# Moving the layer-norm statistics, the normalised rows and the low parts in a decoder kernel

## The chip, the cores and the metric

The kernel runs on one core of one Trainium2 chip. The metric is the device time of one execution in microseconds (us). A core has five engines with an instruction stream each: TensorE (PE in the profile, PEld for its weight loads), VectorE (DVE), ScalarE (ACT), GpSimd (POOL) and SyncE (SP), which only issues DMAs here. They run independently and wait for each other through counting semaphores.

## The reference

The input `x` is 16 sequences of 128 rows by 256. One decoder layer is computed, in three steps that each add to `x` (written out from the reference, with shapes):

```python
xn = layernorm(x)
q = l2norm(xn @ Wq); k = l2norm(xn @ Wk); v = xn @ Wv; a = sigmoid(xn @ Wg)   # 8 heads of 128
S = a_t[..., None] * S + k_t[..., None] * v_t[None, :]     # over the 128 time steps, per head
o_t = S^T q_t
x = x + concat(o) @ Wo                                     # step 1: gated linear attention
xn = layernorm(x)
scores = xn @ (ctx @ W^T)^T ; x = x + softmax(scores) @ ctx   # step 2: cross attention
xn = layernorm(x)
gate = softmax(mean_t(xn) @ gate_w^T); the 2 best of 8 experts per sequence
x = x + sum_k w_k * (gelu(xn @ Wd_k^T + bd_k) @ Wu_k^T + bu_k)   # step 3: experts
```

## The kernel before, in words

**Groups, units and the tail.** Four sequences form a group `i` (0 to 3, `NG = 4`), and a group is worked through head by head. One head of one group is a unit `n = 8i + h` (0 to 31, `U = 32`); "the third head" is `h == 2`, units 2, 10, 18 and 26, and "the fourth" is `h == 3`, units 3, 11, 19 and 27. A unit makes k, g (the gate alpha), q and v by projections on PE, splits the time recurrence into seven levels of products, and folds them into the output rows `o`. On DVE every level needs a decay (`decay`, `decay_first`, `q_decayed`: lines 690, 697, 707, 724), and on ACT a copy of the parts that don't decay (`carry`, `carry_odd_k`: lines 466, 457). Levels 1 to 4 of unit n+1 are prepared while unit n runs, levels 5 and 6 at the start of unit n itself.

The cross attention and the experts of group `t = i - 1` (the tail) are cut into small parts and woven into the units of group `i`. Each engine has its own function `tail_part(n, place)`, which is called at fixed places of the unit and says what the tail does there. So the order of each engine is written out by hand, and the semaphores only make sure that nobody reads too early.

**Layer norm.** Each of the three normalisations runs in three pieces: `ln_variance` on DVE (statistics of four sequences: lines 660, 665, 668), `ln_power` on POOL (the power -1/2: line 371, tile `rstd`), and `ln_normalize` on DVE (four TENSOR_SCALARs that write `xn`: line 676). PE then transposes `xn` by eight matmuls (line 1235), and ACT copies the result out of PSUM (line 497). "mid" names the rows after the attention (`x_mid`, used by the scores), "x" the next group's input rows, "cross" the rows after the cross attention. The next group's transposed rows are kept as a high and a low part: `xT_upper` on ACT copies the high part to `xnT`, and `xT_lower` on DVE subtracts it from the PSUM rows to get the low part (line 809).

**The PSUM ring.** Nearly all that PE makes goes through four PSUM banks in a fixed order, `ORDER` (built at the function `fill_order`). `fill(name)` on PE waits until the engine that reads the fourth-last entry has freed its bank; which semaphore that is stands in `freed_by` (line 232). In unit 11 the entries are: scores, v(11), g(12), q(12), oT(9), k(13), probsT, xT(0), xT(1), o(10), and in unit 12: cross(0), cross(1), v(12), g(13), q(13), oT(10), k(14), o(11), x3T(0), x3T(1), v(13), g(14). Thus xT(0) waits for ACT's square of q(12), o(10) for ACT's square of k(13), cross(1) and v(12) for the two low parts on DVE, g(13) and g(14) for the scaled output rows `o_sb` of heads 10 and 11 (`o_scaled` on DVE, line 770), and q(13) for DVE's residual of cross(0).

**POOL.** In each unit POOL first makes the reciprocal norms of the k and q rows (lines 379 and 382, from `norm_sq`, which DVE writes at line 753 at the start of the unit). Behind them, in the third head, stand the powers of "mid" and of the next "x". `v_scaled` (line 762) needs the reciprocal norms of the k rows.

**DVE in a unit** (the loop at line 965): `norm_floor` (753), `decay(n, 5)` (690), `decay(n, 6)` (697), `v_scaled(n)` (762), tail "early", first decays of the next unit (707, 713, 718, 724), tail "late", five `keep`s (741), decays 2 to 4 of the next unit (690), tail "mid", `o_scaled(n - 1)` (770), tail "end". **ACT in a unit** (the loop at line 572): wide copies to `attnT`, carry 5, tail "early", alpha, block copies, tail "mid", q, oT, k, the carries 1 and 2 of the next unit, tail "carry", carries 3 and 4, tail "end".

Of the kernel before, what the change touches and what calls it, by code (L numbers as in the profile page):

```python
# [38 lines left out]
def decoder_kernel(nc, x, ctx, ctxT, wq, wk, wv, wg, wo, xwT, gateT, expert, up_b,  # L39
# [5 lines left out]
    NG = B // GB  # L45
# [7 lines left out]
    with ExitStack() as stack:  # L53
# [372 lines left out]
        def _(act):  # L426
# [99 lines left out]
            def tail_part(n, place):  # L526
                i, h = divmod(n, H)
                t = i - 1
                at = (h, place)
                if at == (0, "early") and i >= 2:  # L530
                    gelu(i - 2)
                if t >= 0:
                    if at == (2, "carry"):
                        for c in range(KC):
                            tail_to(rowsT[:, c], ("x2T", t, c), x2T_set)
                    if at == (3, "early"):
                        probs_out(t)
                    if at == (3, "carry"):
                        tail_to(probsT[:].rearrange("p b t -> p (b t)"), ("probsT", t, 0), probsT_set)
                    if at == (4, "end"):  # L540
                        for c in range(KC):
                            tail_to(rowsT[:, c], ("x3T", t, c), x3T_set)
                    if at == (6, "mid"):
                        gate_exp_out(t)
                if at == (3, "end") and i + 1 < NG:
                    xT_upper(i + 1)
                if place == "end" and h in (6, 7):
                    tail_to(projT[:, h - 6].rearrange("p b t -> p (b t)"), ("keys", i, h - 6), keys_set)
                if at == (7, "end") and t >= 0:
                    for z in range(2):  # L550
                        downT_out(t, z)
# [99 lines left out]
        def _(dve):  # L651
# [5 lines left out]
            def ln_variance(name, src):  # L657
                at = NORM_AT[name]
                for b in range(GB):
                    last = nc.vector.bn_stats(stats[:, b], src[:, b])  # L660
                last.then_inc(ln_stat, 1)
                wait_first(ln_stat, 2 * at + 1)
                positive(dve, ln_rstd, at)
                for b in range(GB):
                    last = nc.vector.bn_aggr(mean_var[:, b], stats[:, b])
                last.then_inc(ln_stat, 1)
                dve.wait_ge(ln_stat, 2 * at + 2)
                nc.vector.tensor_scalar(var_eps[:], mean_var[:, :, 1], LN_EPS, None, ALU.add).then_inc(ln_var, 1)
# [11 lines left out]
            def decay(n, l):  # L680
                if n > 0:
                    dve.wait_ge(level_mm, LEVELS * (n - 1) + DONE[l if l < INNER else OUTER])
                dve.wait_ge(decayed, OUTER * n + l - 1)
                dve.wait_ge(carry_set, CARRIES * n + min(l - 1, CARRIES))
                dve.wait_ge(span_set, INNER * n + l - 1)
                if l < OUTER:
                    w = 2 ** (l - 1)
                    by = (view(alpha, 1, [[2, 2], [4, N // 4], [0, 2]]) if l == 2 else
                          view(spans, span_at(l - 1), [[1, 2], [2, N // (2 * w)], [0, w]]))
                    nc.vector.tensor_tensor(halves(l, w, True), halves(l - 1, w, True), by, ALU.mult).then_inc(decayed, 1)  # L690
                else:

                    for operand, at, span in ((0, T - BLOCK, 2), (1, 0, 1)):
                        src, dst = (view(states, tile_q(m) + operand * N + at, [[T, GB], [1, BLOCK]])
                                    for m in (l - 1, l))
                        by = view(spans, span_at(l - 1) + span, [[4, GB], [0, BLOCK]])
                        last = nc.vector.tensor_tensor(dst, src, by, ALU.mult)
                    last.then_inc(decayed, 1)
# [57 lines left out]
            def v_scaled(n):  # L756
                pair, half = n // 2, n % 2
                dve.wait_ge(v_mm, n + 1)
                dve.wait_ge(rk_set, 2 * pair + 2)
                positive(dve, o_mm, 2 * pair - 2)  # L760
                by = view(rnorm, (2 * pair - 2) % 4 * 8 + 4 + 2 * half, [[1, 2], [8, 2], [0, P]])
                nc.vector.tensor_tensor(v_sb[:, pair % 2, 2 * half:2 * half + 2],
                                        ring_of(("v", n))[:].rearrange("p (b h v) -> p b h v", b=2, h=2), by,
                                        ALU.mult).then_inc(v_set, 1)
# [9 lines left out]
            def residual(t):  # L774
                positive(dve, out_free, 16 * 2 * t)
                dve.wait_ge(x_in[t % 2], 16 * (t // 2 + 1))
                for z in range(2):
                    dve.wait_ge(wo_mm, 2 * t + z + 1)
                    nc.vector.tensor_tensor(x_mid[:, 2 * z:2 * z + 2], accs[z][:].rearrange("p (b d) -> p b d", b=2),
                                            x_buf[:, t % 2, 2 * z:2 * z + 2], ALU.add).then_inc(mid_set, 1)  # L780
                dve.wait_ge(mid_set, 2 * t + 2)
# [115 lines left out]
            def tail_part(n, place):  # L897
                i, h = divmod(n, H)
                t = i - 1
                at = (h, place)  # L900
                if at == (0, "late") and i >= 2:
                    weigh_up(i - 2)
                if at == (0, "end") and i >= 2:
                    last_residual(i - 2)
                if t >= 0:
                    if at == (1, "end"):
                        residual(t)
                    if at == (2, "early"):
                        ln_variance(("mid", t), x_mid)
                    if at == (2, "late"):  # L910
                        ln_normalize(("mid", t), x_mid, ("x3T", t - 1, 1) if t > 0 else ("xT", 1, 1))
                    if at == (3, "early"):
                        scores_max(t)
                    if at == (3, "end"):
                        probs_rsum(t)
                    if at == (4, "early"):
                        cross_residual(t)
                        dve.wait_ge(cross_set, 2 * t + 2)
                        ln_variance(("cross", t), x_mid)
                if i + 1 < NG:  # L920
                    if at == (2, "end"):
                        dve.wait_ge(x_in[(i + 1) % 2], 16 * ((i + 1) // 2 + 1))
                        ln_variance(("x", i + 1), x_buf[:, (i + 1) % 2])
                    if at == (3, "late"):
                        ln_normalize(("x", i + 1), x_buf[:, (i + 1) % 2], ("x2T", t, 1) if t >= 0 else ("xT", 0, 1))
                    if at == (3, "end"):
                        xT_lower(i + 1)
                if t >= 0:
                    if at == (4, "late"):
                        ln_normalize(("cross", t), x_mid, ("xT", i + 1, 1) if i + 1 < NG else ("x2T", t, 1))  # L930
                    if at == (5, "late"):
                        pool_rows(t)
                        dve.wait_ge(pooled_set, t + 1)
                        gate_products(t)
                    if at == (6, "early"):
                        gate_logits(t)
                    if at == (6, "late"):
                        choose(t)
                    if at == (6, "end"):
                        choice_weights(t)  # L940
# [24 lines left out]
            for n in range(U):  # L965
                if n >= 1:
                    norm_floor(n - 1)
                decay(n, 5)
                decay(n, 6)
                v_scaled(n)  # L970
                tail_part(n, "early")
                if n + 1 < U:
                    decay_first(n + 1)
                    span_products(n + 1)
                    q_decayed(n + 1)
                tail_part(n, "late")
                for k in range(KEEPS):
                    keep(n, k)
                if n + 1 < U:
                    for l in range(2, INNER):  # L980
                        decay(n + 1, l)
                tail_part(n, "mid")
                if n >= 1:
                    o_scaled(n - 1)
                if n == 0:
                    dve.wait_ge(w_in, N_W)
                tail_part(n, "end")
# [505 lines left out]
```

## Time and profile before

| | us |
|---|---|
| median of 3 runs | 513.37 (513.32 to 513.6) |
| the profiled execution | 512.21 |
| its span, first to last instruction | 510.4 |
| PE busy | 467.0 (92% of the span) |
| DVE busy | 365.9 (72%) |
| ACT busy | 338.2 (66%) |
| POOL busy | 110.3 (22%) |

The profile is of one execution. All clock times below count from the start of its span. "Busy" is the time in which an engine executes an instruction; an idle gap in front of an instruction is given in brackets at the end of its row, with the engine that ended it. The mean clock that TensorE was granted is 0.974 of full speed. Parts of the trace differ by group: unit 10 begins at about 146 us, unit 18 at 263 us, unit 26 at 381 us.

### The profile page before, as it was taken

How to read it: one execution, taken by the hardware profiler on the slowest of the kernel's cores; microseconds unless marked ns; L12 is line 12 of the kernel's file. 1: busy time of each engine (PE TensorE's matmuls, PEld its weight loads, DVE VectorE, ACT ScalarE, POOL GpSimd, SP SyncE). 2: the span in 40 equal slices, each digit the busy share in tenths (PEclk: the TensorE clock that was granted, in tenths of full speed). 3: DMA queues.
4: the chain of work that ended last, by engine and by line, in shares of the span. 5: the costliest groups of instructions: out<-in, count | busy, mean ns of one | idle time of the engine just before them, and what ended most of it. 6: DMA issues, size and time to landing. Idle time of an engine off the chain costs nothing.

```text
span 510.4 us, 23866 instructions
## 1 busy us (share of the span) xinstructions
PE 467.0 (92%) x10212; PEld 385.4 (76%) x10212; DVE 365.9 (72%) x1058; ACT 338.2 (66%) x797; POOL 110.3 (22%) x102
## 2 busy tenths in 40 slices
PE   1799999999998899999998899999998999989556
PEld 1587888877887788778887788788887888767345
DVE  5778976666687788774677688774777688773661
ACT  4778677766776848788475867778566867656311
POOL 1023211111122021241122121142021121230130
PEclk9999999999999999999998999999999999999956
DMA  8900000001010010021110010022100010020121
GB/s 324 315 4 3 4 3 4 3 4 44 4 44 3 3 45 4 23 72 38 45 44 3 3 44 4 3 66 64 44 3 3 3 44 4 5 84 3 41 71 53
DMA packets 15256, 20.15 MB, mean 39 GB/s; under 512 B 1200, under 2 KB 12976, under 8 KB 15152
## 3 DMA queue, kind: packets, MB, share of 16 engines
q1 hardware_dynamic: 13872, 14.43, 8.8%
q0 software_dynamic: 1280, 4.20, 2.7%
q8 instruction: 81, 1.33, 1.1%
q14 instruction: 23, 0.19, 0.1%
HBM read 16.53 MB, written 2.10 MB: 37 GB/s over the span
## 4 chain that ended last, share of the span: by engine, by line
PE 69%; DVE 16%; issue 5%; ACT 5%; POOL 2%; DMA 1%; DVEq 0%; ACTq 0%; POOLq 0%
PE ring L1115 20%; PE acc L1226 9%; PE ring L1128 8%; PE lo_bank L1139 7%; PE ring L1207 5%; PE hi_bank L1198 3%; PE ring L1277 2%; PE ring L1214 2%; DVE xn L676 2%; PE ring L1235 2%; DVE states L690 2%; PE hi_bank L1170 1%; DVE spans L718 1%; PE ring L1295 1%; PE ring L1244 1%
## 5 line engine op out<-in xcount | busy, mean ns | idle before, releaser
L466 ACT COPY states<-states 128x512 f32<-128x512 f32 x128 | 80.7, 630 | 46.3 <-DVE states L690 33.4
L379 POOL TENSOR_TENSOR rnorm<-norm_sq,neg_half 128x4 f32<-128x4 f32 x32 | 47.0, 1469 | 269.7 <-DVE norm_sq L753 269.7
L690 DVE TENSOR_TENSOR states<-states,spans 128x512 f32<-128x512 f32 x96 | 66.5, 692 | 7.7 <-ACT states L466 0.3
L1139 PEld LDWEIGHTS lo_bank<-states 128*32 128x32 f32 x5120 | 50.9, 110 | 22.8 <-issue 18.7
L1226 PE MATMUL acc<-wo_sb,oT_sb 128*128 128x256 f32 x256 | 61.9, 385 | 0.7 <-ACT oT_sb L493 0.7
L1139 PE MATMUL lo_bank<-states 128*32 128x16 f32 (+1 forms) x5120 | 57.6, 188 | 0.0
L741 DVE COPY_PREDICATED blocks<-owned,lo_bank 128x64 f32<-128x64 uint32 (+1 forms) x160 | 41.1, 257 | 21.8 <-PE lo_bank L1139 17.2
L1128 PE MATMUL ring<-wv_sb,xnT 128*128 128x256 f32 x384 | 54.5, 291 | 1.4 <-DVE wv_sb L946 1.4
L1115 PE MATMUL ring<-xnT,wk_sb 128*128 128x512 f32 x192 | 53.7, 416 | 2.1 <-DVE xnT L809 1.6
L1115 PE MATMUL ring<-xnT,wq_sb 128*128 128x512 f32 x192 | 53.5, 414 | 0.0
L1226 PEld LDWEIGHTS acc<-wo_sb,oT_sb 128*128 128x128 f32 x256 | 47.2, 194 | 6.2 <-ACT oT_sb L493 0.9
L1115 PE MATMUL ring<-xnT,wg_sb 128*128 128x512 f32 x192 | 50.3, 397 | 0.3 <-DVE wg_sb L946 0.3
L1128 PEld LDWEIGHTS ring<-wv_sb,xnT 128*128 128x128 f32 x384 | 48.1, 188 | 2.0 <-DVE wv_sb L946 1.5
L1115 PEld LDWEIGHTS ring<-xnT,wk_sb 128*128 128x128 f32 x192 | 34.8, 193 | 8.9 <-issue 1.9
L478 ACT COPY attnT<-hi_bank 32x64 f32<-32x64 f32 x128 | 26.0, 203 | 22.4 <-PE hi_bank L1198 15.7
L1115 PEld LDWEIGHTS ring<-xnT,wg_sb 128*128 128x128 f32 x192 | 34.0, 189 | 7.0 <-DVE wg_sb L946 1.1
L1115 PEld LDWEIGHTS ring<-xnT,wq_sb 128*128 128x128 f32 x192 | 33.7, 189 | 7.2
L488 ACT COPY attnT<-blocks 32x128 f32<-32x128 f32 x128 | 37.4, 292 | 1.1
L1207 PE MATMUL ring<-v_sb,attnT 128*128 128x128 f32 x256 | 36.1, 285 | 0.4 <-issue 0.2
L1207 PEld LDWEIGHTS ring<-v_sb,attnT 128*128 128x128 f32 x256 | 32.0, 193 | 5.2 <-issue 4.5
L430 ACT ACTIVATE alpha<-ring 128x512 f32<-128x512 f32 x32 | 19.1, 598 | 25.1 <-PE ring L1115 24.8
L382 POOL TENSOR_TENSOR rnorm<-norm_sq,neg_half 128x4 f32<-128x4 f32 x32 | 33.3, 1041 | 2.4 <-DVE norm_sq L753 2.4
(157 smaller groups left out, 782.9 us busy)
## 6 DMA issues: line engine op xcount, KB each, us to landing
x_buf<-x_dram SPq DMA_DIRECT2D x4, 512.0 KB, 3.9
ctxT_sb<-ctxT_dram SPq DMA_DIRECT2D x8, 256.0 KB, 3.9
ctx_sb<-ctx_dram SPq DMA_DIRECT2D x4, 512.0 KB, 4.0
out_dram<-x_mid SPq DMA_DIRECT2D x6, 256.0 KB, 2.3
states<-wk_dram SPq DMA_DIRECT2D x1, 1024.0 KB, 5.6
states<-wg_dram SPq DMA_DIRECT2D x1, 1024.0 KB, 7.7
states<-wq_dram SPq DMA_DIRECT2D x1, 1024.0 KB, 9.8
v_sb<-wv_dram SPq DMA_DIRECT2D x1, 1024.0 KB, 11.8
```

The costliest lines, as they stand in the source:

```text
L379: nc.gpsimd.tensor_tensor(rnorm[:, m % 4, GB:2 * GB], norm_sq[:, GB:2 * GB], neg_half[:, GB:2 * GB], ALU.pow).then_inc(rk_set, 1)
L382: nc.gpsimd.tensor_tensor(rnorm[:, m % 4, 0:GB], norm_sq[:, 0:GB], neg_half[:, 0:GB], ALU.pow).then_inc(rq_set, 1)
L466: nc.scalar.copy(halves(l, 2 ** (l - 1), False), halves(l - 1, 2 ** (l - 1), False)).then_inc(carry_set, 1)
L478: nc.scalar.copy(by_parity[lo:lo + BLOCK, :, m, lo + BLOCK:lo + 2 * BLOCK], near[at:at + BLOCK])
L488: last = nc.scalar.copy(attnT[lo:lo + BLOCK, :, lo:lo + BLOCK], blocks[lo:lo + BLOCK])
L690: nc.vector.tensor_tensor(halves(l, w, True), halves(l - 1, w, True), by, ALU.mult).then_inc(decayed, 1)
L741: nc.vector.copy_predicated(view(blocks, to, natural), view(owned, k * N_IN + to, natural).bitcast(U32), view(lo_bank, at, order)).then_in ...
L1115: last = mm(dst[:], w[:, a, c, P * h:P * h + P], xnT[:, i % 2, b, c], start=(c == 0 and k == 0), stop=(c == KC - 1 and k == 2))
L1128: last = mm(dst[:, 2 * P * k:2 * P * k + 2 * P], xnT[:, i % 2, a, c, T * b:T * b + T], wv_sb[:, w, c, 2 * P * pair:2 * P * pair + 2 * P], ...
L1139: last = mm(lo_bank[BLOCK * r:BLOCK * r + BLOCK, to:to + columns], view(states, left + start, [[1, BLOCK]]), view(states, right + start, q ...
L1207: last = mm(dst[:, P * b:P * b + P], attnT[:, b], v_sb[:, n // 2 % 2, b, n % 2], start=True, stop=True)
L1226: last = mm(accs[z][:, D * m:D * m + D], oT_sb[:, n % 2, T * b:T * b + T], wo_sb[:, h], start=(h == 0 and m == 0), stop=(h == H - 1 and m ...
```

## The change

The change only moves work; no instruction is added or taken away, on any engine.

```diff
 # ACT, tail_part
-                if at == (3, "end") and i + 1 < NG:
+                if at == (3, "carry") and i + 1 < NG:
                     xT_upper(i + 1)
 # DVE, tail_part
+                    if at == (2, "first"):
+                        ln_variance(("mid", t), x_mid)
                     if at == (2, "early"):
-                        ln_variance(("mid", t), x_mid)
-                    if at == (2, "late"):
                         ln_normalize(("mid", t), x_mid, ("x3T", t - 1, 1) if t > 0 else ("xT", 1, 1))
...
-                    if at == (3, "late"):
+                    if at == (3, "early"):
                         ln_normalize(("x", i + 1), x_buf[:, (i + 1) % 2], ("x2T", t, 1) if t >= 0 else ("xT", 0, 1))
-                    if at == (3, "end"):
+                    if at == (3, "mid"):
                         xT_lower(i + 1)
 # DVE, the loop over units
-                decay(n, 5)
-                decay(n, 6)
-                v_scaled(n)
+                if n % H == 2 and n > H:
+                    tail_part(n, "first")
+                    v_scaled(n)
+                    decay(n, 5)
+                    decay(n, 6)
+                else:
+                    decay(n, 5)
+                    decay(n, 6)
+                    v_scaled(n)
```

The new first place and the new order of v and the two decays are in units 10, 18 and 26. The moves in the fourth head are in units 3, 11 and 19 (group 3 has no next group).

On DVE in unit 10, before, the statistics of `x_mid` stand behind norm_floor (L753), the two wide decays (L690, L697) and v (L762), and the normalised rows `xn` (L676) behind all first decays of unit 11:

```order
L660 BN_STATS stats<-x_mid 128x6 x4
L655 MEMSET scratch 128x1
L665 BN_AGGR mean_var<-stats 128x2 x4
L668 TENSOR_SCALAR var_eps<-mean_var 128x4
L707 TENSOR_TENSOR states<-states,alpha 128x256
L713 TENSOR_TENSOR alpha<-alpha 128x256
L718 TENSOR_TENSOR spans<-alpha 128x128
L718 TENSOR_TENSOR spans<-spans 128x64
L718 TENSOR_TENSOR spans<-spans 128x32
L718 TENSOR_TENSOR spans<-spans 128x16
L724 TENSOR_TENSOR states<-states,alpha 128x512
L676 TENSOR_SCALAR xn<-x_mid,mean_var,rstd 128x256 x4
```

In the change the same place begins with norm_floor (L753) and reads:

```order
L753 TENSOR_SCALAR norm_sq<-hi_bank 128x8
L660 BN_STATS stats<-x_mid 128x6 x4
L655 MEMSET scratch 128x1
L665 BN_AGGR mean_var<-stats 128x2 x4
L668 TENSOR_SCALAR var_eps<-mean_var 128x4
L762 TENSOR_TENSOR v_sb<-ring,rnorm 128x512
L690 TENSOR_TENSOR states<-states,spans 128x2x16x16
L697 TENSOR_TENSOR states<-states,spans 128x4x32 x2
L676 TENSOR_SCALAR xn<-x_mid,mean_var,rstd 128x256 x4
L707 TENSOR_TENSOR states<-states,alpha 128x256
```

The statistics are now ahead of v, v is ahead of the two wide decays, and `xn` stands before L707, the first of the first decays.

On DVE in unit 11, before, the next group's rows `xn` stand behind the first decays; the list begins with the maximum of the scores (L785, L788):

```order
L785 TENSOR_REDUCE row_max<-ring 128x4
L788 TENSOR_SCALAR neg_max<-row_max 128x4
L707 TENSOR_TENSOR states<-states,alpha 128x256
L713 TENSOR_TENSOR alpha<-alpha 128x256
L718 TENSOR_TENSOR spans<-alpha 128x128
L718 TENSOR_TENSOR spans<-spans 128x64
L718 TENSOR_TENSOR spans<-spans 128x32
L718 TENSOR_TENSOR spans<-spans 128x16
L724 TENSOR_TENSOR states<-states,alpha 128x512
L676 TENSOR_SCALAR xn<-x_buf,mean_var,rstd 128x256 x4
```

In the change:

```order
L785 TENSOR_REDUCE row_max<-ring 128x4
L788 TENSOR_SCALAR neg_max<-row_max 128x4
L676 TENSOR_SCALAR xn<-x_buf,mean_var,rstd 128x256 x4
L707 TENSOR_TENSOR states<-states,alpha 128x256
L713 TENSOR_TENSOR alpha<-alpha 128x256
L718 TENSOR_TENSOR spans<-alpha 128x128
L718 TENSOR_TENSOR spans<-spans 128x64
L718 TENSOR_TENSOR spans<-spans 128x32
L718 TENSOR_TENSOR spans<-spans 128x16
L724 TENSOR_TENSOR states<-states,alpha 128x512
L741 COPY_PREDICATED blocks<-owned,lo_bank 128x128
```

`xn` stands right behind the maximum of the scores; the first decays follow it, and the five keeps (L741) come directly behind L724.

At the end of unit 11 two engines change. On ACT the two copies of the high parts (`xnT`) move ahead of the carries 3 and 4 (the last two L466; the first line is carry 2):

```order
 L466 COPY states<-states 128x2x128x2
 L497 COPY probsT<-ring 128x512
-L466 COPY states<-states 128x2x64x4
-L466 COPY states<-states 128x2x32x8
 L497 CAST xnT<-ring 128x512 x2
+L466 COPY states<-states 128x2x64x4
+L466 COPY states<-states 128x2x32x8
 L478 COPY attnT<-hi_bank 32x2x32 x2
```

and on DVE the low parts (L809) move ahead of the scaled output rows (L770) and of the reciprocal of the softmax sum (L792):

```order
 L690 TENSOR_TENSOR states<-states,spans 128x2x64x4
 L690 TENSOR_TENSOR states<-states,spans 128x2x32x8
+L809 TENSOR_TENSOR xnT<-ring,xnT 128x512 x2
 L770 TENSOR_TENSOR o_sb<-ring,rnorm 128x512
 L792 RECIPROCAL prob_rsum<-prob_sum 128x4
-L809 TENSOR_TENSOR xnT<-ring,xnT 128x512 x2
```

PE, POOL and SP execute the same instructions in the same order as before.

## Rows read from the trace of the kernel before

**Rows 1.** The page: clock in 40 slices; ACT's carries (mean ns behind busy us).
```profile
PEclk9999999999999999999998999999999999999956
...
L466 ACT COPY states<-states 128x512 f32<-128x512 f32 x128 | 80.7, 630 | 46.3 <-DVE states L690 33.4
```

**Rows 2.** Waits of PE, 40 to 440 us: total, times, longest (us).
```profile
PE ring L1235 <- DVE xn L676: 9.3, 5, 1.9
```

**Rows 3.** Timeline of PE, units 10 to 13: start, us, instructions, [idle <-releaser].
```profile
151.77 1.04 PE L1139 MATMUL lo_bank<-states 128*32 128x16 f32 x96
...
154.72 1.09 PE L1235 MATMUL ring<-ident,xn 128*128 128x128 f32 x8 [1.91 <-DVE xn L676]
...
171.78 1.09 PE L1235 MATMUL ring<-ident,xn 128*128 128x128 f32 x8 [1.80 <-DVE xn L676]
...
178.12 1.77 PE L1128 MATMUL ring<-wv_sb,xnT 128*128 128x256 f32 x12
...
192.70 1.67 PE L1115 MATMUL ring<-xnT,wg_sb 128*128 128x512 f32 x6
```

**Rows 4.** Timeline of DVE in unit 10.
```profile
146.43 0.17 DVE L753 TENSOR_SCALAR norm_sq<-hi_bank 128x8 f32<-128x8 f32 x1
...
148.26 0.69 DVE L762 TENSOR_TENSOR v_sb<-ring,rnorm 128x512 f32<-128x512 f32 x1 [0.37 <-issue]
...
148.87 1.40 DVE L660 BATCH_NORM_STATS2 stats<-x_mid 128x6 f32<-128x256 f32 x4
...
150.89 0.43 DVE L707 TENSOR_TENSOR states<-states,alpha 128x256 f32<-128x256 f32 x1
...
153.29 1.38 DVE L676 TENSOR_SCALAR xn<-x_mid,mean_var,rstd 128x256 f32<-128x256 f32 x4
```

**Rows 5.** Timeline of POOL in unit 10.
```profile
148.14 1.00 POOL L382 TENSOR_TENSOR rnorm<-norm_sq,neg_half 128x4 f32<-128x4 f32 x1
...
150.96 1.22 POOL L371 TENSOR_TENSOR rstd<-var_eps,neg_half 128x4 f32<-128x4 f32 x1 [1.82 <-DVE var_eps L668]
...
160.86 1.01 POOL L371 TENSOR_TENSOR rstd<-var_eps,neg_half 128x4 f32<-128x4 f32 x1 [8.67 <-DVE var_eps L668]
```

**Rows 6.** Timeline of DVE in units 11 to 13.
```profile
161.09 0.17 DVE L753 TENSOR_SCALAR norm_sq<-hi_bank 128x8 f32<-128x8 f32 x1 [0.31 <-ACT attnT L480]
...
162.94 0.69 DVE L762 TENSOR_TENSOR v_sb<-ring,rnorm 128x512 f32<-128x512 f32 x1 [0.37 <-PE ring L1128]
...
167.92 0.43 DVE L707 TENSOR_TENSOR states<-states,alpha 128x256 f32<-128x256 f32 x1 [3.49 <-ACT alpha L430]
...
175.89 1.26 DVE L809 TENSOR_TENSOR xnT<-ring,xnT 128x512 fp32r<-128x512 f32 x2
...
178.14 0.17 DVE L753 TENSOR_SCALAR norm_sq<-hi_bank 128x8 f32<-128x8 f32 x1 [0.99 <-issue]
...
191.97 0.68 DVE L770 TENSOR_TENSOR o_sb<-ring,rnorm 128x512 f32<-128x512 f32 x1
```

**Rows 7.** Timeline of ACT in unit 11.
```profile
169.49 0.60 ACT L439 ACTIVATE squares<-ring 128x512 f32<-128x512 f32 x1
...
170.92 0.64 ACT L449 ACTIVATE squares<-ring 128x512 f32<-128x512 f32 x1
...
175.08 1.07 ACT L497 CAST xnT<-ring 128x512 fp32r<-128x512 f32 x2
```

**Rows 8.** Timeline of PE: L1226 in units 10 and 18.
```profile
156.55 1.89 PE L1226 MATMUL acc<-wo_sb,oT_sb 128*128 128x256 f32 x8
...
273.57 3.11 PE L1226 MATMUL acc<-wo_sb,oT_sb 128*128 128x256 f32 x8
```

**Rows 9.** Windows: us, busy PE, PEld, DVE, ACT, POOL, then PEclk, DMA, GB/s.
```profile
272.00:277.00 5.00, 5.00 (x53) 4.17 (x55) 4.68 (x16) 2.30 (x4) 0.00 (x0) 0.66 0.00 0
...
464.00:484.00 20.00, 13.55 (x73) 10.50 (x71) 12.09 (x41) 7.15 (x20) 2.81 (x4) 1.00 0.08 27
```

**Rows 10.** Timeline of DVE, start of unit 27.
```profile
395.70 0.17 DVE L753 TENSOR_SCALAR norm_sq<-hi_bank 128x8 f32<-128x8 f32 x1 [2.24 <-issue]
```

## The prediction

> **What bounds the kernel now.** I read the page first. PE is busy 92% of the span, and no other engine is above 72%, so outside the start and the end PE's own instructions are the time, and only what stops PE or slows its clock can be won. Its clock stands at nine tenths or more in all slices but the 22nd and the last two [rows 1].
>
> Then the waits of PE between the start and the last units. One line holds nearly all: five waits, 9.3 us together and none over 1.9, at the transposes of L1235 for `xn` of L676 [rows 2]. The timeline places them: one in unit 10 (1.91 us) for the "mid" rows, one in unit 11 (1.80) for the next group's rows [rows 3], the same pair in units 18 and 19, and the last in unit 26. Unit 3, where `xn` also moves, has none.
>
> Then DVE before such a wait. In unit 10 it hardly rests: from norm_floor at 146.43 to `xn` at 153.29 it has one gap of 0.37 us, in front of v [rows 4]. PE has its 96 matmuls behind it at 151.77 + 1.04 = 152.81 and gets `xn` at 154.72 [rows 3]. DVE does 2.4 us of first decays (150.89 to 153.29, [rows 4]) before `xn`, and nobody is that short of them.
>
> **The "mid" rows in units 10, 18 and 26.** Worked out for unit 10, from the end of norm_floor, 146.43 + 0.17 = 146.60 [rows 4]:
> - The statistics with their small operations take 150.89 - 148.87 = 2.02 us, to 148.62.
> - v could start at 148.26 and is not waited for any more: 148.87 - 148.26 = 0.61, to 149.23.
> - The two wide decays took 148.26 - 0.37 - 146.60 = 1.29, to 150.52.
> - `xn` takes 1.38, to 151.90. That is 0.9 us before PE asks at 152.81, so the wait of 1.91 goes.
>
> The order adds a wait: `xn` is now directly behind POOL's power, with all first decays of unit 11 behind it. POOL ends the second reciprocal at 148.14 + 1.00 = 149.14, and the power takes 1.01 to 1.22, to 150.15 to 150.36 [rows 5]; DVE asks at 150.52. I cost it at nothing. The first decays now start 1.0 later (151.9 instead of 150.89), but what follows `xn` and decays together starts 0.37 earlier than before, since the gap in front of v is filled. Carry 2 on ACT waits for these decays, to 151.9 + 2.4 = 154.3, and the copy of the transposed rows stands behind it: carry 2 takes 0.63 [rows 1], the two copies some 1.1 like the two of rows 7, so they end at 156.0. PE reads them behind L1226, which ended at 156.55 + 1.89 = 158.44 [rows 8], now 156.5. It just fits, and costs nothing.
>
> What speaks against this is a rule of the Trainium skill (SBUF — State Buffer, "Who interferes with whom"): a VectorE instruction with two inputs in SBUF and a GpSimd instruction that reads SBUF exclude each other for their whole length. The new place sets the power beside just such decays. The trace has the same power at 1.22 beside the first decays and at 1.01 in unit 11 with DVE nearly idle [rows 5], a difference of 0.21 and no full block. By the row `xn` waits for nothing; by the rule POOL might start at 150.5 only and end at 151.5, 1.0 later, which is a rival below.
>
> **The next rows in units 11 and 19.** Up to the maximum of the scores DVE saves its three gaps 0.37, 0.31 and 0.37 [rows 4, 6], since the 1.9 us that PE is ahead lets v and norm_floor find their inputs ready: about 1.0 us. The exponentials, the table load and alpha follow on ACT, all 1.0 earlier. `xn` now fills part of the 3.49 us in which DVE waits for alpha [rows 6], so it is ready near 165, far before PE needs it, and the wait of 1.80 for it goes too.
>
> It does not follow that PE gets 1.80. The ring is late next. The first transposed bank needs the square of q(12), which ended at 169.49 + 0.60 = 170.09, and the bank of o(10) the square of k(13), which ended at 170.92 + 0.64 = 171.56 [rows 7]. Both come 1.0 earlier. So PE, which was ready for the transposes at 171.78 - 1.80 = 169.98 [rows 3] and could be there at 168.1, starts them at 169.1 and o(10) at 170.6. Before, o(10) could start at 171.78 + 1.09 = 172.87 [rows 3]. Of 1.91 + 1.80 = 3.71 us PE keeps 2.3.
>
> Then DVE is next. The two high parts (1.07 us, [rows 7]) stand before carry 3, and decay 4 needs carry 3. From the square of k at 170.6, ACT has the odd carry, carry 2 and the copy of probsT, at up to 0.63 each [rows 1] say 1.7, then 1.07, then carry 3 with 0.63: 174.0. Decay 4 (0.7, like the other 128x512 operations) ends at 174.7, the low parts (1.26, [rows 6]) at 175.9, the scaled output rows at 176.5, and norm_floor starts at 176.6 instead of 178.14 [rows 6]. DVE's lead is 1.5 us. The second low part frees the bank of v(12) at 175.9, and PE, 2.3 ahead of 178.12 [rows 3], gets there at 175.8: with the output rows still ahead of the low parts it would have waited 0.7 more, so that move pays for itself there. The bounds of these two moves: between 0, if other waits hide them, and 1.07 + 1.26 = 2.3 us of DVE's lead, if they hide behind nothing; my walk has them in full on the path, less the 0.99 gap in front of norm_floor that they fill.
>
> PE must fall back to DVE's lead. In unit 13, g(14) started at 192.70, and the scaled rows of head 11, for which its bank waits, ended at 191.97 + 0.68 = 192.65 [rows 3, 6]. There is no slack. So each of groups 1 and 2 keeps 1.5 us, not 2.3.
>
> **The last group, unit 26.** No next rows follow, and DVE waits 2.24 us at the start of unit 27 for ACT, which waits for PE [rows 10]. DVE has slack there and moves with PE: the whole wait is won, 1.9 us. Unit 3: PE waited for nothing; 0.
>
> **The clock.** Right behind the wait of unit 18, PE was busy for all of 272 to 277 us at a mean granted clock of 0.66, the lower level of 1.2 GHz in its middle, and 5 x 0.34 = 1.7 us went [rows 9]; L1226 took 3.11 us there and 1.89 in unit 10 [rows 8]. It happened behind one of five equal waits. I take it that without the waits it does not happen, and keep 0 and 3.4 us (a second one in the runs that were not profiled, which are slower) as ends.
>
> **Sum.** 1.5 + 1.5 + 1.9 + 1.7 = 6.6 us. Against the profiled execution, 512.21 us (span 510.4 and 1.8 around it), that is 505.6. The median of the runs is 1.16 higher, so 506.8.
>
> **Rivals.**
> - Both waits count in full and the clock holds: 9.3 + 1.7 = 11.0, 502.4 us. For it: PE is 92% busy and most banks are free in time. Against: the two squares and the row of g(14) above. 8%.
> - The clock falls all the same, once, somewhere else: 4.9, 508.5 us. For it: the fall came behind one wait in five, so what precedes it is not fixed by the wait alone. 15%.
> - POOL's power is held up by the decays: `xn` ends at 152.9 instead of 151.9, just in time for PE, but DVE is 1.0 us later in units 10 and 18, and 0.5 is left of its 1.5 there: 4.6, 508.8 us. Against: [rows 5]. 8%.
> - Slower: in the last part PE is busy 13.55 of the 20 us from 464 to 484 at full clock [rows 9], and at half clock behind it [rows 1]. All of it starts 6.6 us sooner, and what set the moment of the fall is not in the trace. If it comes 10 us earlier, half of the 13.55 doubles on the path: 6.8 us back, 513.6; at 464 it is all of it, 520.3. It decides if the fall comes before about 474. Against: the gaps of the last part stay as they are. 5%.
> - The change does not do what it says, because something not seen here (a wait of v for its norms, the table load) holds DVE in each of the units: 513. 2%.
>
> **How the numbers follow.** 62% are left for the forecast, whose own range is 505.3 to 508.0. The range for all is 504.3 to 509.6: the unknown DVE lead moves it by 1.6, the clock by 1.7 each way. A difference below 0.2% (1.0 us) can't be told from none here. Faster by more: the forecast, the first three rivals, 0.92 or so; within: 0.02; slower: 0.06.
>
> **What would show it.** PE has no wait for L676 left after the start. In unit 10 `xn` starts near 150.5 and L1235 near 152.8. In unit 11 the idle time in front of L1235 is ended by ACT's square of q and is under 1 us; a new short wait stands in front of the o rows (L1207). In unit 13 a new wait of some 0.5 us stands in front of g(14), for L770. The clock stands at nine tenths in the 22nd slice too. The prediction is wrong if DVE waits for L371 in front of `xn`, if PE's lead at unit 13 is above 2 us or below 1, or if the clock falls elsewhere.

## The result, and the profile after

The changed kernel takes 506.1 us (median of 4 runs, 504.39 to 506.75), the kernel before 513.35 beside it (512.98 to 513.6). The ratio is 0.9847, 95% interval 0.9822 to 0.9873: faster by 1.5%, and 0.7 us from the forecast of 506.8. The profiled execution took 506.75 us (span 504.9), against 512.21 (span 510.4).

The waits of TensorE between 40 and 440 us (total, times, longest), after. They answer to [rows 2]; L1241 is the old L1235, L1213 the o rows, L1121 the projections:

```profile
PE ring L1241 <- ACT squares L439: 1.2, 2, 0.6
PE ring L1213 <- ACT squares L449: 0.5, 2, 0.3
PE ring L1121 <- DVE v_sb L762: 0.5, 1, 0.5
```

The 9.3 us for `xn` are gone. What stands there instead are the two squares of the ring, as the prediction had them, 1.7 us in all. The 0.5 for v (L762) is in the trace of before too.

Before times of the two traces are compared, one thing has to be taken off. All of unit 10 stands 2.35 us later after than before, though no instruction ahead of 40 us changed. The starts of the o rows of heads 8 and 28, before and then after (timeline of PE):

```profile
140.75 1.16 PE L1207 MATMUL ring<-v_sb,attnT 128*128 128x128 f32 x8
...
431.39 1.16 PE L1207 MATMUL ring<-v_sb,attnT 128*128 128x128 f32 x8
```

```profile
143.10 1.16 PE L1213 MATMUL ring<-v_sb,attnT 128*128 128x128 f32 x8
...
425.39 1.16 PE L1213 MATMUL ring<-v_sb,attnT 128*128 128x128 f32 x8
```

The windows of after show why (us, busy PE, PEld, DVE, ACT, POOL, then PEclk): a stretch at half clock before 31 us, none where [rows 9] has one, and a new one past 452.

```profile
23.00:31.00 8.00, 6.65 (x145) 5.53 (x134) 6.36 (x10) 3.19 (x6) 2.95 (x2) 0.57 0.19 57
270.00:277.00 7.00, 7.00 (x142) 6.50 (x141) 6.55 (x23) 5.46 (x14) 0.15 (x1) 1.00 0.01 2
452.00:458.00 6.00, 5.50 (x61) 5.23 (x61) 1.23 (x1) 3.28 (x12) 0.00 (x0) 0.72 0.01 3
```

From here on a kernel's **inner gain** is meant: how much shorter its way from o(8) to o(28) is than before's 431.39 - 140.75 = 290.64 us, with the time at half clock on that way (busy time times the share of clock missing: before 1.7) taken off on both sides. For the change: 290.64 - 1.7 - (425.39 - 143.10) = 6.7 us.

DVE in unit 10, after (answers to [rows 4]):

```profile
148.77 0.17 DVE L753 TENSOR_SCALAR norm_sq<-hi_bank 128x8 f32<-128x8 f32 x1
148.85 1.40 DVE L660 BATCH_NORM_STATS2 stats<-x_mid 128x6 f32<-128x256 f32 x4
...
150.81 0.69 DVE L762 TENSOR_TENSOR v_sb<-ring,rnorm 128x512 f32<-128x512 f32 x1
...
152.60 1.38 DVE L676 TENSOR_SCALAR xn<-x_mid,mean_var,rstd 128x256 f32<-128x256 f32 x4
```

There is no gap, neither in front of v nor of `xn`. Less 2.35, `xn` starts at 150.25, where the prediction had 150.52. POOL beside it (answers to [rows 5]):

```profile
149.02 1.01 POOL L379 TENSOR_TENSOR rnorm<-norm_sq,neg_half 128x4 f32<-128x4 f32 x1 [9.63 <-DVE norm_sq L753]
150.00 1.00 POOL L382 TENSOR_TENSOR rnorm<-norm_sq,neg_half 128x4 f32<-128x4 f32 x1
150.97 1.00 POOL L371 TENSOR_TENSOR rstd<-var_eps,neg_half 128x4 f32<-128x4 f32 x1
```

PE, after (answers to [rows 3]): the transposes in unit 10 without a wait, those of unit 11 behind the square of q, the o rows behind the square of k, and g(14).

```profile
155.09 1.09 PE L1241 MATMUL ring<-ident,xn 128*128 128x128 f32 x8
...
171.13 1.11 PE L1241 MATMUL ring<-ident,xn 128*128 128x128 f32 x8 [0.60 <-ACT squares L439]
172.50 1.16 PE L1213 MATMUL ring<-v_sb,attnT 128*128 128x128 f32 x8 [0.27 <-ACT squares L449]
...
192.75 1.67 PE L1121 MATMUL ring<-xnT,wg_sb 128*128 128x512 f32 x6
```

DVE in units 11 to 13, after (answers to [rows 6]): `xn` has taken 1.3 us of the wait for alpha, and decay 4 waits 1.28 us for carry 3, which is behind the two copies on ACT. The profile names PE's products L1176 as releaser, but in copies late below decay 4 starts ahead of them (at 176.10, they at 176.51), so it is not they that hold it.

```profile
163.84 0.68 DVE L762 TENSOR_TENSOR v_sb<-ring,rnorm 128x512 f32<-128x512 f32 x1
...
168.81 0.43 DVE L707 TENSOR_TENSOR states<-states,alpha 128x256 f32<-128x256 f32 x1 [2.19 <-ACT alpha L430]
...
175.86 0.69 DVE L690 TENSOR_TENSOR states<-states,spans 128x512 f32<-128x512 f32 x1 [1.28 <-PE hi_bank L1176]
176.47 1.28 DVE L809 TENSOR_TENSOR xnT<-ring,xnT 128x512 fp32r<-128x512 f32 x2
...
178.35 0.13 DVE L753 TENSOR_SCALAR norm_sq<-hi_bank 128x8 f32<-128x8 f32 x1
...
192.01 0.68 DVE L770 TENSOR_TENSOR o_sb<-ring,rnorm 128x512 f32<-128x512 f32 x1
```

### The profile page after: what moved, and what is told of

Read it like the earlier page. It is cut to its first block, busy times and chain, and to the rows that moved or that the text cites. A ratio compares the mean times of both kernels' runs of the same rounds, so it can differ in the third digit from the quotient of the medians.

```text
span 504.9 us, 23866 instructions
## 1 busy us (share of the span) xinstructions
PE 469.6 (93%) x10212; PEld 387.0 (77%) x10212; DVE 364.5 (72%) x1058; ACT 337.8 (67%) x797; POOL 107.7 (21%) x102
## 4 chain that ended last, share of the span: by engine, by line
PE 49%; DVE 9%; ACT 5%; issue 4%; POOL 1%; DMA 1%; ACTq 0%; DVEq 0%; POOLq 0%
PE ring L1121 13%; PE acc L1232 7%; PE ring L1134 5%; PE lo_bank L1145 5%; PE ring L1213 4%; PE hi_bank L1204 2%; PE ring L1283 2%; PE ring L1220 2%; PE ring L1301 1%; PE ring L1267 1%; PE hi_bank L1176 1%; DVE states L690 1%; PE ring L1293 1%; DVE stats L660 1%; ACT probs L507 1%
## 5 line engine op out<-in xcount | busy, mean ns | idle before, releaser
L466 ACT COPY states<-states 128x512 f32<-128x512 f32 x128 | 80.9, 632 | 46.8 <-DVE states L690 31.2
L379 POOL TENSOR_TENSOR rnorm<-norm_sq,neg_half 128x4 f32<-128x4 f32 x32 | 44.8, 1400 | 267.9 <-DVE norm_sq L753 267.9
L690 DVE TENSOR_TENSOR states<-states,spans 128x512 f32<-128x512 f32 x96 | 66.4, 692 | 10.0 <-PE hi_bank L1176 2.5
L1232 PE MATMUL acc<-wo_sb,oT_sb 128*128 128x256 f32 x256 | 60.7, 380 | 0.7 <-ACT oT_sb L493 0.7
L741 DVE COPY_PREDICATED blocks<-owned,lo_bank 128x64 f32<-128x64 uint32 (+1 forms) x160 | 41.0, 256 | 22.2 <-PE lo_bank L1145 17.6
L1134 PE MATMUL ring<-wv_sb,xnT 128*128 128x256 f32 x384 | 55.7, 295 | 1.3 <-DVE wv_sb L946 1.3
L1121 PE MATMUL ring<-xnT,wk_sb 128*128 128x512 f32 x192 | 53.7, 416 | 2.0 <-DVE xnT L809 1.6
L1121 PE MATMUL ring<-xnT,wq_sb 128*128 128x512 f32 x192 | 53.4, 413 | 0.0
L1121 PE MATMUL ring<-xnT,wg_sb 128*128 128x512 f32 x192 | 51.8, 406 | 0.4 <-DVE wg_sb L946 0.3
L1134 PEld LDWEIGHTS ring<-wv_sb,xnT 128*128 128x128 f32 x384 | 49.2, 193 | 1.9 <-DVE wv_sb L946 1.4
L1121 PEld LDWEIGHTS ring<-xnT,wk_sb 128*128 128x128 f32 x192 | 34.8, 193 | 8.9 <-issue 1.9
L1121 PEld LDWEIGHTS ring<-xnT,wg_sb 128*128 128x128 f32 x192 | 34.9, 194 | 7.4 <-DVE wg_sb L946 1.1
L1121 PEld LDWEIGHTS ring<-xnT,wq_sb 128*128 128x128 f32 x192 | 33.7, 189 | 7.1
L1213 PE MATMUL ring<-v_sb,attnT 128*128 128x128 f32 x256 | 35.7, 282 | 0.6 <-ACT squares L449 0.5
L1213 PEld LDWEIGHTS ring<-v_sb,attnT 128*128 128x128 f32 x256 | 31.6, 191 | 5.8 <-issue 4.0
L382 POOL TENSOR_TENSOR rnorm<-norm_sq,neg_half 128x4 f32<-128x4 f32 x32 | 33.7, 1052 | 2.4 <-DVE norm_sq L753 2.4
```

The lines of the kernel that those rows point to most:

```text
L379: nc.gpsimd.tensor_tensor(rnorm[:, m % 4, GB:2 * GB], norm_sq[:, GB:2 * GB], neg_half[:, GB:2 * GB], ALU.pow).then_inc(rk_set, 1)
L382: nc.gpsimd.tensor_tensor(rnorm[:, m % 4, 0:GB], norm_sq[:, 0:GB], neg_half[:, 0:GB], ALU.pow).then_inc(rq_set, 1)
L466: nc.scalar.copy(halves(l, 2 ** (l - 1), False), halves(l - 1, 2 ** (l - 1), False)).then_inc(carry_set, 1)
L741: nc.vector.copy_predicated(view(blocks, to, natural), view(owned, k * N_IN + to, natural).bitcast(U32), view(lo_bank, at, order)).then_in ...
L1121: last = mm(dst[:], w[:, a, c, P * h:P * h + P], xnT[:, i % 2, b, c], start=(c == 0 and k == 0), stop=(c == KC - 1 and k == 2))
L1134: last = mm(dst[:, 2 * P * k:2 * P * k + 2 * P], xnT[:, i % 2, a, c, T * b:T * b + T], wv_sb[:, w, c, 2 * P * pair:2 * P * pair + 2 * P], ...
```

## The experiments

Ten further measurements, one of them of the unaltered change. Each ratio is to the kernel before measured beside it, whose runs spread from 511.8 to 516.9 us, so the medians tell half a per cent at best, and medians of kernels that were not measured beside each other are not compared. The inner gain of the trace tells more: the unaltered change has 6.7 in one trace and 6.4 in another, so about 0.3 us is what it can't tell.

| kernel | median us | ratio to before (95%) | inner gain us |
|---|---|---|---|
| the change | 506.1 | 0.9847 (0.9822 to 0.9873) | 6.7 |
| third head only | 509.73 | 0.992 (0.9883 to 0.9957) | 4.9 |
| fourth head only | 511.01 | 0.9947 (0.9916 to 0.9978) | 1.7 |
| statistics late | 508.84 | 0.9897 (0.9862 to 0.9933) | 2.1 |
| output rows first | 504.83 | 0.9846 (0.9793 to 0.9898) | 5.4 |
| maximum first | 501.59 | 0.9753 (0.97 to 0.9807) | 10.0 |
| copies late | 506.29 | 0.9834 (0.9784 to 0.9884) | 6.4 |
| v behind | 504.72 | 0.983 (0.9769 to 0.9891) | 6.1 |
| rows late | 509.08 | 0.9916 (0.9885 to 0.9948) | 3.3 |
| the change again | 504.02 | 0.9807 (0.9759 to 0.9856) | 6.4 |
| start filled | 504.95 | 0.9839 (0.9771 to 0.9908) | 6.3 |

**Third head only.** The three moves in the fourth head are undone.

```diff
-                if at == (3, "carry") and i + 1 < NG:      # ACT
+                if at == (3, "end") and i + 1 < NG:
...
-                    if at == (3, "early"):                 # DVE, ln_normalize of x
+                    if at == (3, "late"):
...
-                    if at == (3, "mid"):                   # DVE, xT_lower
+                    if at == (3, "end"):
```

> Only the moves in the third head are kept (statistics of the mid rows ahead of v, v ahead of the wide decays, mid rows ahead of the first decays); the fourth head is as before. Theory A (the ring's squares and VectorE limit what two waits give together): the wait for L676 in unit 11 comes back and grows, since TensorE arrives 2.0 us sooner and VectorE only about 1.0: some 2.8 us of it. Start of the o rows against before, freed of clock differences: 2.0 us earlier at o(9), 1.0 at o(10); over all three groups 1.0 + 1.0 + 2.0 = 4.0 us. Theory B (the waits are independent, each edit is worth its own wait): 1.9 in each group, 5.7 us.

PE's waits between 40 and 440 us, and the timeline of PE in unit 11:

```profile
PE ring L1241 <- DVE xn L676: 4.2, 2, 2.1
```

```profile
171.72 1.97 PE L1241 MATMUL ring<-ident,xn 128*128 128x128 f32 x8 [2.12 <-DVE xn L676]
```

2.0 us are won at o(9). The wait in unit 11 does grow, but from 1.80 to 2.12 only, not to 2.8: `xn` is ready there 1.5 us sooner against o(8), where A gave DVE 1.0. In the three groups 1.6, 1.4 and 1.9 are kept: 4.9 us, half way between A's 4.0 and B's 5.7. A has the mechanism and overrates it. The transposes took 1.97 instead of 1.09 us there, since the clock fell, behind a wait for `xn` as in unit 18 of before (window as in [rows 9], granted clock 0.72):

```profile
171.00:177.00 6.00, 5.29 (x27) 4.80 (x27) 5.52 (x15) 4.29 (x9) 0.00 (x0) 0.72 0.01 3
```

**Fourth head only.** The kernel before with those three moves.

> Only the moves in the fourth head are kept (next rows ahead of the first decays, high parts ahead of carries 3 and 4, low parts ahead of the output rows); the third head is as before. Theory A: the waits of 1.9 us in units 10, 18 and 26 stay, the waits in units 11 and 19 go, but o(10) can't start before the square of k at 171.6 on the clock of before, against 172.87: 1.2 us in each of two groups, 2.4 us in all. Theory B: 1.8 us in each, 3.6. Theory C (what the whole change shows over its third head alone): 0.3 in each, 0.6.

```profile
PE ring L1235 <- DVE xn L676: 5.8, 3, 1.9
PE ring L1207 <- ACT squares L449: 0.5, 2, 0.3
PE ring L1235 <- ACT squares L439: 0.5, 2, 0.3
```

Three of five waits stay, the squares appear. o(10) starts 1.1 us sooner against o(8), and 0.8 and 0.9 are kept: 1.7 us where A said 2.4, B 3.6 and C 0.6. A's 1.2 counted from 172.87, the end of the transposes of before, but o(10) started at 172.71. With the third head's 4.9 this makes 6.6, the whole change: the parts add up, but each is worth less than its own waits (1.9 + 1.9 + 1.9 and 1.8 + 1.8).

**Statistics late.** In units 10, 18 and 26 the two wide decays, v, and only then the statistics.

```diff
-                if n % H == 2 and n > H:
-                    tail_part(n, "first")
-                    v_scaled(n)
-                    decay(n, 5)
-                    decay(n, 6)
-                else:
-                    decay(n, 5)
-                    decay(n, 6)
-                    v_scaled(n)
+                decay(n, 5)
+                decay(n, 6)
+                v_scaled(n)
+                if n % H == 2 and n > H:
+                    tail_part(n, "first")
```

> The whole change, but with the two wide decays, then v, then the statistics, and the mid rows directly behind them, so that POOL's power has nothing of VectorE's to hide behind. Theory A: VectorE waits about 1.2 us for L371 in front of the rows in units 10, 18 and 26; TensorE waits for L676 again, 0.8 us in each; VectorE is 1.4 us later in unit 11, so the start of o(10) is only 0.5 earlier than before. In all 0.5 + 0.5 + 1.1 = 2.1 us faster than before without the clock, 4.8 slower than the whole change. Theory B (the place of the statistics does not matter, only the rows ahead of the decays): within 0.5 us of the whole change.

DVE in unit 10, then the waits of PE:

```profile
154.66 1.38 DVE L676 TENSOR_SCALAR xn<-x_mid,mean_var,rstd 128x256 f32<-128x256 f32 x4 [1.12 <-POOL rstd L371]
```

```profile
PE ring L1216 <- ACT probs L507: 2.0, 2, 1.0
PE ring L1237 <- DVE xn L676: 1.8, 3, 0.6
```

2.1 us of inner gain, as A said; B is out. The wait for POOL is there (1.12), and `xn` starts 1.75 us later against o(8) than in the change. The later DVE in unit 11, which A had only as delay, shows as a wait of its own: the bank of oT(9), which the exponentials free, 1.0 in each of two groups.

**Rows late.** The statistics stay ahead of v, but the mid rows are behind the first decays again (`"late"` for the `"early"` of `ln_normalize` in the third head).

> The whole change, but the mid rows are behind the first decays again in units 10, 18 and 26 (the statistics stay ahead of v). Theory A: the filled gap of 0.37 us is all that is won in those units, TensorE waits 1.5 us for L676 in each; in units 11 and 19 the other moves are worth 0.9 plus that 0.37; in all 3 x 0.4 + 2 x 0.9 = 3.0 us faster than before without the clock, 3.7 slower than the whole change. Theory B (the early statistics are what ends the wait): within 1 us of the whole change.

```profile
PE ring L1241 <- DVE xn L676: 3.8, 3, 1.3
```

3.3 us, A's 3.0. Against fourth head only, with its 1.7, the early statistics (with v ahead of the decays) are worth 1.6 us, the early rows alone (statistics late) 0.4, and both together 4.9 or 5.0: each needs the other.

**v behind.** In the third head the order is statistics, decays, v, rows.

> The whole change, but in units 10, 18 and 26 v stands behind the two wide decays again (statistics, decays, v, rows). Theory A: the sum of VectorE's work before the rows is the same and v is not waited for so early: the same within 0.2 us, without the clock. Theory B (v must be ahead, since its bank or POOL needs it): some 0.5 us slower in each of three groups.

The inner gain is 6.1, that is 0.3 and 0.6 below the two traces of the change; A has it at 0 below, B at 1.5. PE in unit 10, v behind; k(12) starts 0.63 behind the transposes of o here, and 0.36 behind them after (152.17 and 152.53). DVE ends v at about 151.4, behind the start of the rows at 151.33, and v's bank is the one that k(12) takes.

```profile
150.84 0.60 PE L1216 MATMUL ring<-ident,o_sb 128*128 128x128 f32 x4
151.47 1.67 PE L1117 MATMUL ring<-xnT,wk_sb 128*128 128x512 f32 x6
```

So v ahead of the decays is worth about 0.27 us a time in front of k(12); units 18 and 26 show the same 0.63 and 0.64. It is the bank that B named, at half of B's price, and over the three groups hardly more than the inner gain can tell.

The order has a second effect. With v behind, the power of the mid rows starts beside a wide decay and not beside v. DVE and POOL, v behind:

```profile
149.54 0.69 DVE L690 TENSOR_TENSOR states<-states,spans 128x512 f32<-128x512 f32 x1
```

```profile
149.63 1.47 POOL L371 TENSOR_TENSOR rstd<-var_eps,neg_half 128x4 f32<-128x4 f32 x1
```

It takes 1.47 us, against 1.00 in the change. It ends at 151.10, and the rows start at 151.33 without a wait for it. So the rival of the prediction in which the decays hold up POOL's power can happen, at 0.47 and not 1.0 us, and here it would still be hidden.

**Output rows first.** The low parts are behind the output rows again (`"end"` for the `"mid"` of `xT_lower`).

> The whole change, but the low parts of the next rows are again behind the scaled output rows and the reciprocal (VectorE, units 3, 11 and 19). Theory A: the second low part frees the bank of v(12) 0.7 us later, TensorE waits there about 0.5 us, so 0.4 in each of two groups, 0.9 us in all slower than the whole change. Theory B: this move is worth nothing, since other waits cover it: within 0.2.

```profile
PE ring L1267 <- DVE xnT L809: 0.8, 2, 0.4
```

The inner gain falls by 1.0 to 1.3 us to 5.4; A (0.9) holds in size. The wait, 0.4 a time, is one entry earlier than A had it, in front of cross(1), whose bank the first low part frees. The ratio, 0.9846, is that of the change, 0.9847, and the traced execution was even 1.9 us shorter than the change's (504.87 and 506.75): it had no half clock before 470 us. Neither tells what the move does.

**Copies late.** The high parts are behind carries 3 and 4 again on ACT (`"end"` for `"carry"`).

> The whole change, but the high parts of the next rows are again behind carries 3 and 4 on ScalarE. Theory A: decay 4 no longer waits 1.28 us for carry 3, but the low parts on VectorE then wait for the high parts; the second low part ends within 0.7 us of where it ended and the bank of v(12) has that slack, so within 0.3 us of the whole change, without the clock. Theory B (the early copies are what makes the move of the low parts possible): cross and v(12) wait for the low parts, 0.5 in each of two groups, 1.0 us slower.

DVE in unit 11:

```profile
176.10 0.69 DVE L690 TENSOR_TENSOR states<-states,spans 128x512 f32<-128x512 f32 x1 [0.31 <-ACT states L466]
177.14 1.29 DVE L809 TENSOR_TENSOR xnT<-ring,xnT 128x512 fp32r<-128x512 f32 x2 [0.35 <-ACT xnT L497]
```

6.4 us: the same, as A said. The wait of 1.28 for carry 3 becomes two of 0.3. The move on ACT is worth nothing.

**Maximum first.** The change, and in units 11, 19 and 27 the maximum of the scores ahead of the wide decays and v.

```diff
-                    if at == (3, "early"):
+                    if at == (3, "first"):
                         scores_max(t)
...
                 else:
+                    if n % H == 3 and n > H:
+                        tail_part(n, "first")
                     decay(n, 5)
```

> The whole change, and in units 11, 19 and 27 the maximum of the scores (L785, L788) moves ahead of the two wide decays and v on VectorE. Theory A (in units 11 and 19 the ring waits for ScalarE's squares, which stand behind the exponentials and the table load, which stand behind the maximum): ScalarE starts 1.8 us sooner, the waits of 0.6 for the square of q and 0.27 for the square of k go, o(10) starts 0.9 sooner than in the whole change, the same in unit 19, nothing in unit 27: 1.8 to 2.0 us in all, without the clock. Theory B (what is left in unit 11 is VectorE's own work, which is not shorter): no change, within 0.3.

ACT in unit 11, then PE (o(8) is at 142.30 in this trace, 0.8 sooner than in that of the change):

```profile
162.64 0.37 ACT L507 ACTIVATE probs<-ring,neg_max 128x128 f32<-128x128 f32 x1
...
167.67 0.60 ACT L439 ACTIVATE squares<-ring 128x512 f32<-128x512 f32 x1
```

```profile
169.61 1.04 PE L1243 MATMUL ring<-ident,xn 128*128 128x128 f32 x8
170.48 1.06 PE L1215 MATMUL ring<-v_sb,attnT 128*128 128x128 f32 x8
```

Both waits for squares are gone, and the square of q comes 1.9 us sooner against o(8) (167.67 - 142.30, against 170.38 - 143.10). The gain is 3.3 us over the change, more than A's 2.0: 1.2 by o(10), 1.5 kept in each of two groups, 0.3 in unit 27. It is all kept, and the 0.26 that the change loses up to g(14) with it, because DVE's lead grows too: the output rows that free the bank of g(14) start at 189.74, 1.47 sooner against o(8) than in the change (192.01). With a ratio of 0.9753 (0.97 to 0.9807) this kernel is the fastest measured here.

**The change again, and start filled.** The second adds useless transposes of the identity into the accumulator bank, which is not used yet, where PE rests before 25 us.

```diff
+            def keep_warm(count):
+                for _ in range(count):
+                    nc.tensor.transpose(acc0[:, 0:P], ident[:], ident[:])
...
+            keep_warm(16)          # ahead of the wait for ln_out
...
+            keep_warm(6)           # ahead of the wait for w_split 1
...
+            keep_warm(8)           # ahead of norms(-1)
...
+            keep_warm(8)           # behind norms(-1)
```

> The whole change, unaltered, once more. Theory A (the place where the granted clock falls before 40 us differs from execution to execution and has nothing to do with the change): the start of the o rows from o(10) to o(28), read against the same kernel's own o(8), is as in its first trace within 0.2 us, while o(2) may stand anywhere from 65.3 to 69 us. Theory B (the change itself costs 2.3 us at the start): o(2) stands at 67.8 again, within 0.2.

> The whole change, and TensorE does useless transposes of the identity into the unused accumulator bank where it is idle before 25 us: 16 ahead of the first rows, 6 ahead of k(0), 8 ahead of and 8 behind the norms of the second k. Theory A (the clock falls there because TensorE rests at 21 to 25 us): no half clock between 23 and 31 us, and o(2) stands at 65.5 us or sooner in the trace; the median is 1 to 2 us below that of the whole change run beside it. Theory B (the moment of the fall does not depend on these rests): o(2) scatters as before and the median is the same or up to 1 us above, for the added work.

The window of 23 to 31 us, the change again, then start filled:

```profile
23.00:31.00 8.00, 6.80 (x150) 5.98 (x151) 6.99 (x12) 3.67 (x7) 2.95 (x2) 0.79 0.20 62
```

```profile
23.00:31.00 8.00, 7.92 (x161) 6.28 (x161) 7.53 (x17) 4.53 (x8) 2.94 (x2) 1.00 0.22 64
```

The unaltered kernel lost less there the second time (clock 0.79, not 0.57), and o(2) started at 66.79 instead of 67.76: theory B of the first, that the change itself costs 2.3 us at the start, is out. Filled, the clock held and o(2) started at 64.49, as A says. But the clock also held there without filling in the traces of before and of output rows first, two of eleven. And the medians, 504.95 and 504.02 with ranges of 502.5 to 509.55 and 502.92 to 506.88, show no gain where A had 1 to 2 us. Whether the filling or chance held the clock stays open.

## Why the prediction was right

The waits went and came as forecast, and the time lies in the range. But the parts of the sum are less good than the total. Two of the three signs by which the prediction called itself wrong came true: TensorE's lead at unit 13 is 2.3 us, above 2, and in the traced execution the clock fell elsewhere. The total is near 506.8 because the two errors have opposite signs, and that is luck.

**The mid rows.** Right in place and size: `xn` at 150.25 against 150.52, L1241 at 155.09 - 2.35 = 152.74 against 152.8, no wait for POOL. 2.0 us were won at o(9) and 2.0 kept in unit 26, where 1.9 was forecast. Statistics late and rows late show that the pair does it together.

**The next rows.** The ring took over as forecast: 0.60 for the square of q, 0.27 for the square of k. o(10) started at 172.50 - 2.35 = 170.15, forecast 170.6, so against 172.71 of before 2.6 us were won there, not 2.3. The term at fault is DVE's "about 1.0" by the maximum of the scores: v, just ahead of it, started at 163.84 - 2.35 = 161.49 and not at 162.94, 1.45 sooner, and the squares on ACT came 1.46 sooner. Some 0.3 of the missing 0.4 was there at norm_floor of unit 11 already (162.44 - 2.35 against 161.09, 1.0 sooner where the walk's gaps give 0.68). The walk put each piece behind the end of the one before, while on DVE the next can start a little earlier (norm_floor of unit 10 ends at 148.94, the statistics start at 148.85); in unit 10 that made `xn` 0.27 sooner than forecast.

**DVE's lead.** This is the term that was mis-sized: 1.5 us kept in each of groups 1 and 2, measured 2.3 and 2.4. Norm_floor of unit 12 started at 178.35 - 2.35 = 176.0, not 176.6, so DVE's lead was 2.1 there. The chain on ACT was put right: from the end of the square of k to the start of decay 4 the walk has 3.4 us, and the trace 175.86 - 172.45. It only began 0.5 sooner, by the term above:

```profile
171.81 0.64 ACT L449 ACTIVATE squares<-ring 128x512 f32<-128x512 f32 x1
```

By g(14) DVE was 2.3 ahead (192.01 against 191.97 with the shift of 2.35). The limit itself is there: the output rows end at 192.01 + 0.68 = 192.69 and g(14) starts at 192.75. Up to g(14) 0.26 of the 2.56 us were lost, not 0.8, and the wait of 0.5 that I announced is 0.1 to 0.2.

**The moves at the end of the fourth head.** Low parts ahead of the output rows: I said they save 0.7 in each group at v(12), output rows first shows 0.5 to 0.6. High parts ahead of the carries: nothing, as the bounds allowed.

**The clock.** The fall behind the wait of unit 18 did not come again in the middle of any trace without such waits. Of those with them, third head only had one, and fourth head only, statistics late and rows late had none. But I took one fall in the middle as the clock's whole part. The traced execution had one at the start and one near 455 us instead, so the second rival, a fall somewhere else, is in part what happened in it: 6.7 + 1.7 for the fall that went, less 2.3 at the start and 1.7 near 455, is 4.4. The rest is in the last part, from o(28) to the end: the half clock there cost 6.8 us before and 6.1 after (windows of 1 us), and what is left is 0.6 shorter. That is why this execution won 5.5 us and not 6.6. In the medians, 7.2 us apart, the two errors of the sum nearly cancel: 6.7 us of inner gain instead of 4.9, and 0.5 from all else instead of 1.7. That no term of the clock is in the medians is inferred from this difference; the executions without a trace don't show where their clock fell.

**The rivals.** Both waits in full (11.0): no, 6.7. POOL held up by the decays (4.6): no, the power took 1.00 behind the reciprocals, since it started beside v; v behind shows what it takes beside a decay. Slower by an earlier half clock: no; in each of the twelve traces it set in 26 to 28 us before the end, as before.

## What to carry to other kernels

When a wait of the busiest engine is removed, look at the ring of buffers for what frees the next bank: here 9.3 us of waits were worth 6.7, and the next limit, the maximum ahead of the exponentials, was worth another 3.3. Moving a consumer forward only pays together with its producer (the statistics and the rows). And when the clock makes executions of one kernel differ by 4 us, compare the way between two fixed instructions in the traces, with the time at half clock taken off, before believing a median.

## What the runs showed of the hardware

The first power of a unit on POOL (L379) took 1.49 us in unit 10 of before, beside a wide decay of DVE that had started 0.07 us ahead of it, and 1.01 us after, beside the statistics; both after 9.6 us of rest. The same holds throughout: between 60 and 450 us of before, 26 of the 27 first powers took 1.48 to 1.55 us, each with a wide decay started 0.04 to 0.07 ahead; the 27th (161.83) began 0.54 behind the start of its decay, with 0.15 of it left, and took 1.02. Before, DVE and POOL:

```profile
146.61 0.69 DVE L690 TENSOR_TENSOR states<-states,spans 128x512 f32<-128x512 f32 x1
```

```profile
146.68 1.49 POOL L379 TENSOR_TENSOR rnorm<-norm_sq,neg_half 128x4 f32<-128x4 f32 x1 [9.66 <-DVE norm_sq L753]
```

So the neighbour costs the half microsecond, not the rest. The loss is what was left of the decay when the power began, less about 0.15: 146.61 + 0.69 - 146.68 = 0.62 left and 0.48 lost here; in [rows 4] and [rows 5] 150.89 + 0.43 - 150.96 = 0.36 left and 0.21 lost; in v behind 0.60 left and 0.46 lost.

That agrees with the rule that the prediction weighed (the Trainium skill, SBUF — State Buffer, "Who interferes with whom"): the decay has two inputs in SBUF, the statistics have one, and the one that starts first holds the other up. In the other direction the traces do not bear the rule out, and they decide: after, the decay behind v ran for its usual time though a power of 1.00 us was under way since 150.97, where an exclusion for the whole instruction would have held it until 151.97:

```profile
151.42 0.68 DVE L690 TENSOR_TENSOR states<-states,spans 128x512 f32<-128x512 f32 x1
```

The same is in unit 11 of before, whose power the prediction read as beside an idle DVE: a wide decay started 0.43 us into it (161.29 against 160.86), and the power took 1.01 and the decay 0.69.
